# Front of a sequence three ahead in the tail of a step, and pass two's causal mask as a product over 64 rows on TensorE

## The chip, the cores and the metric

One core of one Trainium2 chip. The time is device microseconds of one execution, from the program's first to its last instruction on the core. TensorE is called PE, VectorE DVE, ScalarE ACT, GpSimd POOL and SyncE SP.

## The reference, cut to what matters

32 sequences of 256 tokens with 128 channels go through a layer norm and then through two branches that are added to x: a 16-head attention with rotary positions and a distance bias, and a block with routed projections (8 experts, a gate from cosine similarity), causal attention and a mixture of experts.

```python
xn = layernorm(x)
# branch A: 16 heads of 8 channels
q_rot, k_rot = rotate(q, cos, sin), rotate(k, cos, sin)
scores = q_rot @ k_rot.T / sqrt(8) - |i - j| / xi[h] * e_gate[h]
attn = softmax(where(causal, scores, -inf)); A = (attn @ v) @ Wo.T
# branch B
n1 = layernorm(xn) * ln1_w + ln1_b
rw = gating(n1)                                   # 8 weights a token
q, k, v = sum_e rw[:, e] * (n1 @ proj[e])         # one head of 128
hs = xn + sum_e rw[:, e] * (softmax(causal(q @ k.T) / sqrt(128)) @ v) @ o_proj[e]
n2 = layernorm(hs); B = hs + sum_e rw2[:, e] * gelu(n2 @ w1[e]) @ w2[e]
out = x + A + B
```

## The kernel before, in words

The 32 sequences are worked off by 32 calls of `step(n, u, n_x)` on every engine, one for each sequence n (u is its parity); 26 of them run in a hardware loop of two steps. After them a last stage does the mixture of experts. Each engine has its own program, and its order is written out by hand; engines meet only at semaphores. n_x says how much lies ahead: 3 in steps 0 to 28, 2 in step 29, 1 in step 30, 0 in step 31.

A step mixes three sequences. For n it does branch B's projections (`qk`, `ve`, `soft_scores`, `soft_T`, `soft_av`, `oe`) and branch A's second pass (`unit2`, exponentials, `pv`, `out_T`, `att_T`, `att_out`). For n+1 it does branch A's first pass (`unit1`: scores whose row maxima DVE takes in `row_max`; `max_parts`, `max_T` and `put_max` bring the maxima back into the stacks as rows of pass two). For n+2 it does the front: `norm_T` (transposes of both norms into bank G0), `proj` (q and k with their rotated partners, one after the other through bank G1), `logits_T`, `logits`, `proj_v`, and on DVE `rotate` and `gating`. DVE also makes the layer norm of n+3.

Branch A's scores come in 6 units for each pass. Pass one uses banks S1 (0, 1); a causal mask is put there first by a product of `mask_l` and `mask_r` over the 64 rows of each of two row groups. Pass two uses banks S2 (2, 3); there ACT writes the mask as a seed (`seed_slot`, L669) after each exponential (`exp_slot`, L663), and PE's `unit2` waits for `seed_done`.

DVE's `gating` is a chain of 31 links; each waits for the one before it. Between links stand other pieces of work, at places given by `beside_gating(k)`: one piece of the next layer norm after each link, and row maxima, `normalise`, `soft_max` and `soft_norm` at fixed k. In `layer_norm` the first piece waits for the sequence's x (`x_in`) and then runs `bn_stats` and `bn_aggr` (L881, L884). In the tail DVE runs `max_parts`, `normalise(n, 1)`, five `scale_att`, `add_x` and `add_hs`. `add_hs` ends with the sum `bs` (L1144) that counts `base_done` up.

SP runs all large transfers in one queue. Its step begins like this (L436, L432):

```python
sp_.wait_ge(base_done, n)
if not isinstance(n, int) or n > 0:
    store_base(n - 1, 1 - u)
load_x(n, u, xr, xr_in)
if n_x == 3:
    sp_.wait_ge(x_in, 16 * (n + 3))
    load_x(n + 3, 1 - u, xt, x_in)
```

Lines that the prediction names: `norm_T` L1313, `proj` L1321, `logits` L1334, `proj_v` L1344, `weights_T` L1354, `unit1`'s masks L1371 and L1374, `max_T` L1393, `unit2` L1408 and L1411, `ve` L1458, `soft_T` L1476, `oe` L1493, `att_T` L1501; on DVE `rotate` L987 to L997, `gating` from L1014, `row_max` L1070; on ACT the copy of xnT L617.

Of the kernel before, what the change touches and what calls it, by code (L numbers as in the profile page):

```python
# [15 lines left out]
S = 256  # L16
# [44 lines left out]
GATE_MAX_AT = (7, 12, 17, 22)  # L61
# [58 lines left out]
def build(nc, x, w_attn, w_o, log_xi, pi_logit, e_logit, ln1_w, ln1_b, ln2_w, ln2_b, sim1, gates1,  # L120
# [9 lines left out]
    with ExitStack() as ctx:  # L130
# [9 lines left out]
        mask_in = sb("mask_in", [P, 2, P])  # L140
        mask_half = sb("mask_half", [P, 4, P])
        mask_qk = sb("mask_qk", [P, 2, P], BF16)
        mask_l = sb("mask_l", [P, P], BF16)
# [79 lines left out]
        seeds = trn[:].rearrange("p a t -> p (a t)").bitcast(BF16).rearrange("p (k t) -> p k t", k=2)  # L223
# [16 lines left out]
        S1, S2, PVB, QKB, G0, G1 = (0, 1), (2, 3), 4, 5, 6, 7  # L240

# [42 lines left out]
        seed_done = sem("seed_done")  # L284
# [69 lines left out]
        def _(sp_):  # L354
# [3 lines left out]
            for dst, src in ((ident[:], c_ident), (mask_in[:, 0], c_mask_qk), (mask_in[:, 1], c_mask_kq),  # L358
                             (theta[:], c_pos_freq), (sin_sign[:], c_sin_sign), (cpos[:], c_pos),
                             (rank[:], c_rank), (lnp[:, 0:1], ln1_w), (lnp[:, 1:2], ln1_b),  # L360
                             (lnp[:, 2:3], ln2_w), (lnp[:, 3:4], ln2_b),
                             (sims[:, 0], sim1), (sims[:, 1], sim2)):
                sp_.dma_start(dst, src).then_inc(ld_const, 16)
# [229 lines left out]
        def _(act):  # L593
# [17 lines left out]
            def evac_norm(b, par):  # L611

                act.wait_ge(xzT_out, b + 1)

                if not isinstance(b, int) or b > 1:
                    act.wait_ge(n1s_done, E * (b - 1))
                act.activation(xnT[:], ps[:, G0, 0:S], ACT.Copy).then_inc(xnT_done, 1)  # L617
                act.activation(n1T[:, par], ps[:, G0, S:2 * S], ACT.Identity, bias=lnp[:, 1:2],
                               scale=lnp[:, 0:1]).then_inc(n1T_done, 1)
                act.wait_ge(n1T_done, b + 1)  # L620
                act.activation(sqT[:, 0:S], n1T[:, par], ACT.Square).then_inc(sq_done, 1)
# [18 lines left out]
            def evac_weights(b):  # L640
                act.wait_ge(rwT_out, b + 1)

                act.wait_ge(rw_stored, 16 * b)
                act.activation(rwT[0:E * T, 0:P], ps[0:E * T, S1[1], 0:P], ACT.Copy).then_inc(rwT_done, 1)

            def evac_max(b):
                act.wait_ge(mT_out, b + 1)
                act.wait_ge(max_in, 16 * NF * b)
                act.activation(mT[:], ps[0:3 * H, S1[0], 0:S // 2].bitcast(BF16), ACT.Copy).then_inc(mT_done, 1)
# [22 lines left out]
            def exps(n, k):  # L672
                exp_slot(n, k)
                seed_slot(n, k)
# [84 lines left out]
            def step(n, u, n_x):  # L759
                if n_x >= 2:  # L760
                    evac_norm(n + 2, u)
                exps(n, 0)
# [5 lines left out]
                exps(n, 1)  # L768
# [3 lines left out]
                exps(n, 2)  # L772
# [5 lines left out]
                exps(n, 3)  # L778
                if n_x == 0:
                    scale_norm2(3)  # L780
                exps(n, 4)
# [10 lines left out]
                if n_x:  # L792
                    seed_slot(n, 5)
# [19 lines left out]
            for b in range(2):  # L813
                evac_norm(b, b)
# [3 lines left out]
                evac_weights(b)  # L818
            evac_max(0)
# [50 lines left out]
        def _(dve):  # L870
# [86 lines left out]
            for h in range(2):  # L957
                ch.add(dve.tensor_copy(mask_qk[:, h], mask_in[:, 0]))
# [5 lines left out]
            ch.add(dve.scalar_tensor_tensor(mask_l[:], mask_half[:, 1], FAINT, mask_half[:, 0], ALU.mult, ALU.add))  # L964
            ch.link(dve.memset(seeds[:, 0], 0.0))
            for h in range(2):
                ch.add(dve.tensor_copy(seeds[:, 0, S * h:S * h + P], mask_in[:, 1]))
            ch.add(dve.tensor_copy(seeds[:, 1].rearrange("p (h t) -> p h t", h=HG),
                                   mask_in[:, 1:2].broadcast_to((P, HG, P))))
# [14 lines left out]
            def rotate(b, beside=None):  # L984
                c = Chain(dve, rot_chain, b, ROT_LINKS, beside)
                dve.wait_ge(rot_q_out, b + 1)
                c.link(dve.tensor_tensor(rott[:, 0], ps[:, G1].rearrange("p (a t) -> p a t", a=2), cs[:, 0], ALU.mult))  # L987
                c.add(dve.tensor_tensor(rot[:, 0], rott[:, 0, 0], rott[:, 0, 1], ALU.add))
                dve.wait_ge(rot_k_out, b + 1)
                c.link(dve.tensor_tensor(rott[:, 1], ps[:, G1].rearrange("p (a t) -> p a t", a=2), cs[:, 1], ALU.mult))  # L990
# [187 lines left out]
            def step(n, u, n_x):  # L1178
# [5 lines left out]
                def beside_rotation(k):  # L1184
                    if k == 1:
                        next_max(0)

# [3 lines left out]
                def beside_gating(k):  # L1191
                    next(norm, None)
                    if k in GATE_MAX_AT:
                        next_max(2 + GATE_MAX_AT.index(k))
                    if k == 11:
                        normalise(n, 0)
                    if k == 14:
                        soft_max(n)
                    if k == 20:
                        soft_norm(n)  # L1200
                if n_x >= 2:
                    rotate(n + 2, beside_rotation)
                    next_max(1)
                    gating(n + 2, T, 0, gate1, LG1, NORM1, 1, beside_gating)
                    run(norm)
                else:
                    for k in range(1, ROT_LINKS + 1):
                        beside_rotation(k)
                    next_max(1)
# [13 lines left out]
                add_x(n, u)  # L1223
                add_hs(n, u)

            for b in range(2):
                norm = layer_norm(b + 1, 1 - b)
                rotate(b)
# [4 lines left out]
            max_parts(0)  # L1233
            step(0, 0, 3)
# [61 lines left out]
        def _(pe):  # L1296
# [5 lines left out]
            for j in range(2):  # L1302
                mm(ps[:, S2[j]], identb[:], seeds[:, 0], start=True, stop=False, skip_group_check=True)
            pe.wait_ge(ld_w, 16 * N_W)

            def norm_T(b, free):
# [4 lines left out]
                for k, src in enumerate((xn[:], zt[:])):  # L1311
                    for i in range(T):
                        ins = pe.transpose(ps[:, G0, (T * k + i) * P:(T * k + i + 1) * P], src[:, i], ident[:])  # L1313
                ins.then_inc(xzT_out, 1)

            def proj(b, side, prev):
# [3 lines left out]
                for k in range(2):  # L1320
                    ins = mm(ps[:, G1, k * S:(k + 1) * S], wa[:, 2 * side + k], xnT[:], start=True, stop=True)  # L1321
# [25 lines left out]
            def weights_T(b, old):  # L1347
                pe.wait_ge(rw_out, 3 * (b + 1))
                if old:

                    pe.wait_ge(s1_read, UNITS * b)
                else:
                    pe.wait_ge(rwT_done, b)
                pe.transpose(ps[0:E * T, S1[1], 0:P], gt[:, 6, 0:T].rearrange("p i e -> p (i e)"), ident[:]  # L1354
                             ).then_inc(rwT_out, 1)

            def unit1(b, par, k):

                Q, i = divmod(k, 3)
                if k == 0:  # L1360

                    pe.wait_ge(rwT_done, b + 1 if not isinstance(b, int) or b else 2)
                    pe.wait_ge(mT_done, b)
# [4 lines left out]
                for f in range(NF):  # L1368
                    bank = ps[:, S1[f]]
                    if i == 0:  # L1370
                        mm(bank, mask_l[ROWS[f]], mask_r[ROWS[f]].rearrange("p h t -> p (h t)"), start=True, stop=False,  # L1371
                           skip_group_check=True)
                    else:
                        mm(bank.rearrange("p (h t) -> p h t", h=2)[:, :, P:S], mask_l[ROWS[f]], mask_r[ROWS[f], 0:2],  # L1374
# [13 lines left out]
            def max_T(b):  # L1388

                pe.wait_ge(max_chain, (MAX_LINKS + 1) * (b + 1))  # L1390
                pv = ps[:, S1[0], 0:S // 2].bitcast(BF16)
# [4 lines left out]
            def unit2(n, u, k):  # L1396
# [4 lines left out]
                if not isinstance(n, int) or UNITS * n + k >= 1:  # L1401
                    pe.wait_ge(seed_done, UNITS * n + k)
# [12 lines left out]
            def pv(n, u, Q):  # L1415
# [4 lines left out]
                if Q == 0:  # L1420
                    pe.wait_ge(v_done, n + 1)
                    pe.wait_ge(xa_done, n)
                for f in range(NF):
# [133 lines left out]
            def step(n, u, n_x):  # L1557
                f = n + 2

                def next_max(k):  # L1560
                    if n_x:
                        unit1(n + 1, 1 - u, k)
# [38 lines left out]
                soft_scores(n, (lambda: pe.wait_ge(rot_chain, ROT_LINKS * f + 3)) if n_x >= 2 else  # L1601
                            (lambda: pe.wait_ge(hs_done, n)))
# [4 lines left out]
                next_max(3)  # L1607
# [5 lines left out]
                next_max(4)  # L1613
# [5 lines left out]
                next_max(5)  # L1619
# [3 lines left out]
                if n_x >= 2:  # L1623
                    weights_T(f, True)
                    proj_v(f, True)
                if n_x:
                    max_T(n + 1)

                att_T(n)
                oe(n, 0)  # L1630
                oe(n, 1)
                att_out(n)
                if n_x == 0:
                    weights_T2(0)
                    logits2_T(1)
                for e in range(2, E):
# [4 lines left out]
            for b in range(2):  # L1641

                norm_T(b, lambda: pe.wait_ge(lg_read, b))
                proj(b, 0, lambda: pe.wait_ge(rot_chain, ROT_LINKS * b))
                logits_T(b, b)
                proj(b, 1, lambda: pe.wait_ge(rot_chain, ROT_LINKS * b + 1))
                logits(b)
                proj_v(b, False)
                weights_T(b, False)

            pe.wait_ge(set_dma, 16 * (N_SMALL + N_ROWS))
            for k in range(UNITS):
# [110 lines left out]
```

## Time and profile before

| | us |
|---|---|
| median of 3 runs | 1389.92 |
| lowest, highest | 1386.5, 1391.0 |
| the profiled execution | 1386.97 |
| its span | 1385.1 |
| PE busy | 1229.1 (89%) |
| DVE busy | 1004.5 (73%) |
| ACT busy | 707.4 (51%) |
| POOL busy | 211.0 (15%) |

The steps lie between about 96 and 1142 us of the span, the last stage behind them. Times in the rows are microseconds from the start of the span. In a row of the timeline the first number is the start, the second the time to the end of the last of the merged instructions; "xN" is their count, and a bracket gives how long the engine was idle before the row and which instruction ended that. A PE row's end is modelled, so here the distance from start to start is used for what PE spends on a row.

### The profile page before, as it was taken

The page shows a single profiled execution, that of the slowest core. Times are in us where ns is not written, and L with a number is a line of the kernel's source. Part 1 is how long each engine was busy: PE and PEld are TensorE (multiplying, and loading weights), DVE is VectorE, ACT ScalarE, POOL GpSimd, SP SyncE. Part 2 cuts the span into 40 slices and gives each one's busy share as a digit, 9 for nine tenths or more (in the row PEclk, how much of TensorE's full clock was granted, in tenths as well). Part 3 has the DMA queues.
Part 4 walks back from the last instruction along what each step waited for, and adds up shares of the span by engine and source line. Part 5 has one row for each costly group of instructions (what it writes and reads, how often), then busy time and mean ns, then how long its engine had stood idle before and what let it go on. Part 6 is the DMA issues. An engine that isn't in the chain of part 4 may idle for free.

```text
span 1385.1 us, 33706 instructions
## 1 busy us (share of the span) xinstructions
PE 1229.1 (89%) x10780; PEld 938.4 (68%) x10780; DVE 1004.5 (73%) x3691; ACT 707.4 (51%) x1281; POOL 211.0 (15%) x325
## 2 busy tenths in 40 slices
PE   1249999999999999999999999999999979999998
PEld 0127777777777677777777777777777766777776
DVE  5547777777777777777777777777777657777653
ACT  1115555555555555555555555555555665555532
POOL 1011111121111222221111111112111200000000
PEclk9659999999999999999999999999999999999999
DMA  5312232222222222222322222222222106544344
GB/s 131 87 63 79 79 90 81 82 82 77 78 78 82 81 80 78 77 77 81 96 97 77 77 79 88 81 82 81 80 80 78 53 26 230 194 154 154 154 169 153
DMA packets 107942, 133.19 MB, mean 96 GB/s; under 512 B 18116, under 2 KB 87252, under 8 KB 99692
## 3 DMA queue, kind: packets, MB, share of 16 engines
q1 hardware_dynamic: 105668, 131.66, 29.6%
q10 hardware_dynamic: 2216, 0.80, 0.2%
q8 instruction: 32, 0.52, 0.2%
q14 instruction: 26, 0.21, 0.0%
HBM read 109.12 MB, written 21.54 MB: 94 GB/s over the span
## 4 chain that ended last, share of the span: by engine, by line
PE 68%; DVE 16%; issue 9%; SPq 4%; DMA 2%; ACT 1%; DVEq 0%; ACTq 0%
PE ps L1448 9%; PE ps L1493 9%; PE ps L1694 8%; PE ps L1449 8%; PE ps L1680 8%; PE ps L1321 4%; PE ps L1458 3%; PE ps L1425 2%; DVE mx L1070 2%; PE ps L1408 2%; SPq L415 2%; PE ps L1371 1%; PE ps L1507 1%; PE ps L1381 1%; DVE xn L894 1%
## 5 line engine op out<-in xcount | busy, mean ns | idle before, releaser
L1070 DVE TENSOR_REDUCE mx<-ps 128x4 f32<-128x1024 f32 (+1 forms) x192 | 234.9, 1223 | 89.4 <-PE ps L1381 80.0
L663 ACT ACTIVATE pr<-ps 128x1024 f32<-128x1024 f32 x192 | 195.8, 1020 | 138.4 <-PE ps L1408 93.7
L558 POOL TENSOR_TENSOR n1s<-rep,n1T 128x256 f32<-128x256 f32 x256 | 176.8, 728 | 254.3 <-DVE mpart L1084 254.3
L669 ACT ACTIVATE ps<-trn 128x1024 f32<-128x1024 bf16 x191 | 197.2, 1032 | 5.1
L1694 PEld LDWEIGHTS ps<-w2s,ats 128*128 128x128 f32 x1024 | 131.7, 192 | 49.8 <-issue 46.8
L1448 PE MATMUL ps<-n1s,wqk 128*128 128x256 f32 x512 | 163.0, 400 | 0.0
L1449 PE MATMUL ps<-n1s,wqk 128*128 128x256 f32 x512 | 152.7, 380 | 0.0
L1458 PE MATMUL ps<-wv,n1s 128*128 128x128 f32 x1024 | 141.6, 281 | 0.0
L1493 PE MATMUL ps<-wop,ats 128*128 128x128 f32 x1024 | 140.0, 294 | 0.0
L842 ACT ACTIVATE n1s<-ps 128x512 f32<-128x512 f32 x128 | 76.5, 597 | 122.6 <-PE ps L1680 121.5
L1694 PE MATMUL ps<-w2s,ats 128*128 128x128 f32 x1024 | 135.7, 276 | 0.5 <-DVE ats L1253 0.5
L1458 PEld LDWEIGHTS ps<-wv,n1s 128*128 128x128 f32 x1024 | 126.7, 191 | 11.5 <-issue 6.5
L1493 PEld LDWEIGHTS ps<-wop,ats 128*128 128x128 f32 x1024 | 131.3, 207 | 4.1 <-issue 0.2
L1680 PE MATMUL ps<-rep,w1s 128*128 128x512 f32 x256 | 130.7, 594 | 0.0
L565 POOL TENSOR_TENSOR zt<-xn,rstd 128x256 f32<-128x256 f32 x32 | 19.6, 612 | 638.2 <-DVE rstd L901 638.2
L1449 PEld LDWEIGHTS ps<-n1s,wqk 128*128 128x128 f32 x512 | 97.6, 191 | 13.4
L1448 PEld LDWEIGHTS ps<-n1s,wqk 128*128 128x128 f32 x512 | 87.2, 190 | 25.9 <-issue 12.5
L617 ACT ACTIVATE xnT<-ps 128x256 f32<-128x256 f32 x32 | 12.3, 383 | 162.6 <-PE ps L1313 144.7
L1121 DVE TENSOR_TENSOR ats<-rep,ps 128x512 f32<-128x512 f32 (+1 forms) x160 | 81.2, 574 | 0.0
L1321 PE MATMUL ps<-xnT,wa 128*128 128x256 f32 x256 | 73.4, 412 | 1.6 <-ACT xnT L617 0.9
L1137 DVE SCALAR_TENSOR_TENSOR hs<-ps,smx,hs 128x128 f32 (+1 forms) x64 | 19.5, 347 | 74.2 <-PE ps L1493 74.2
L1425 PE MATMUL ps<-pr,vst 128*32 128x256 f32 x1024 | 68.5, 385 | 0.4 <-ACT pr L663 0.4
(228 smaller groups left out, 2038.3 us busy)
## 6 DMA issues: line engine op xcount, KB each, us to landing
rep<-scr_rw SPq DMA_DIRECT2D x32, 1024.0 KB, 5.0
stk<-scr_rw SPq DMA_DIRECT2D x16, 1024.0 KB, 8.1
stk<-scr_parts SPq DMA_DIRECT2D x896, 16.0 KB
scr_parts<-parts SPq DMA_DIRECT2D x64, 192.0 KB, 2.3
rots<-scr_rw SPq DMA_DIRECT2D x8, 1024.0 KB, 4.8
wqk<-scr_rw SPq DMA_DIRECT2D x8, 1024.0 KB, 8.9
stk<-scr_parts SPq DMA_DIRECT2D x128, 48.0 KB
xt<-in_x SPq DMA_DIRECT2D x32, 128.0 KB, 2.5
```

The lines of the kernel that those rows point to most:

```text
L558: pool.tensor_tensor(n1s[:, e], rep[:, par, e], n1T[:, par], ALU.mult).then_inc(n1s_done, 1)
L663: act.activation(pr[:, Q, :, i], ps[:, S2[0]:S2[0] + NF], ACT.Exp).then_inc(exp_done, 1)
L669: act.activation(ps[:, S2[0]:S2[0] + NF], seeds[:, kind:kind + 1].broadcast_to((P, NF, 512)), ACT.Copy).then_inc(seed_done, 1)
L1070: dve.tensor_reduce(mx[:, min(i, 1)].rearrange("p (f h) -> p f h", f=NF)[:, :, h:h + n], ps[:, S1[0]:S1[0] + NF].rearrange("p f (h t) -> p ...
L1321: ins = mm(ps[:, G1, k * S:(k + 1) * S], wa[:, 2 * side + k], xnT[:], start=True, stop=True)
L1425: mm(ps[32 * h:32 * h + 32, PVB, 0:S], vst[:, u, 0, HH * f + HG * Q + h], pr[:, Q, f, h // 2, (h % 2) * S:(h % 2 + 1) * S], start=(f == 0) ...
L1448: mm(ps[:, QKB, 0:S], wq[:, e], n1s[:, e], start=(e == 0), stop=(e == E - 1), skip_group_check=True)
L1449: ins = mm(ps[:, QKB, S:2 * S], wk[:, e], n1s[:, e], start=False, stop=(e == E - 1), skip_group_check=True)
L1458: ins = mm(ps[:, QKB, i * D:(i + 1) * D], n1s[:, e, i * P:(i + 1) * P], wv[:, e], start=(e == 0 and i == 0), stop=(e == E - 1), skip_group ...
L1493: ins = mm(ps[:, G1, i * D:(i + 1) * D], ats[:, e, i * P:(i + 1) * P], wop[:, e], start=(e == 0 and i == 0), stop=(e == E - 1), skip_group ...
L1680: mm(ps[:, UP[k % 4]], w1s[:, e], n2T[t % 8], start=True, stop=True).then_inc(up_out, 1)
L1694: ins = mm(ps[:, MOE[t % 2], i * D:(i + 1) * D], hgs[:, k % 2, i * P:(i + 1) * P], w2s[:, e], start=(e == 0 and i == 0), stop=(e == E - 1) ...
```

## The change

1. The front of a sequence is worked three ahead in place of two ahead. In steps 0 to 28, `norm_T(n+3)` and `proj(n+3, 0)` (q) stand in PE's tail behind `proj_v(n+2)`, and `proj(n+3, 1)` (k) behind `oe(n, 3)`. They use the banks `LATER` = S1[0] for the transposes, S1[1] for q, PVB for k, where before it was G0, G1, G1. ACT's `evac_norm` is split: xnT is copied in the tail (`evac_norm_x`), n1T and its square at the start of the next step (`evac_norm_1`). DVE's `rotate(n+3)` stands between `add_x(n)` and `add_hs(n)`. The start of the step loses them. The setup does the same once for sequence 2, and step 29 has no front of its own to transpose or project.
2. `weights_T` and `max_T` go to bank G1 in place of S1, and PE waits for ACT's copies of both (`rwT_done`, `mT_done`) ahead of `oe(n, 0)`, which writes the same bank. `evac_weights` waits for `mT_out`.
3. Pass two's mask is a product on PE (`mask_r` as the stationary side, `mask_q` as the moving one) ahead of each `unit2`; `seed_slot` and its semaphore go, and `unit2` waits for the exponential of the unit before.
4. The six row maxima of n+1 all stand beside the gating chain, at k = 2, 7, 11, 16, 20, 24; before, two stood beside or behind `rotate` and four at k = 7, 12, 17, 22. `soft_max` moves from k = 14 to 17, `normalise(n, 0)` from 11 to 18, `soft_norm` from 20 to 28. PE's `unit1` calls move with them, 2 to 5 each to an earlier place.
5. The setup loses two seeds' tiles and PE's two products with them, and one constant load. SP's program is as before but for that load.

```diff
-GATE_MAX_AT = (7, 12, 17, 22)
+GATE_MAX_AT = (2, 7, 11, 16, 20, 24)
+        FIRST, LATER = (G0, G1, G1), (S1[0], S1[1], PVB)
@@ ACT
-            def evac_norm(b, par):
+            def evac_norm_x(b, banks):
                 act.wait_ge(xzT_out, b + 1)
+                act.activation(xnT[:], ps[:, banks[0], 0:S], ACT.Copy).then_inc(xnT_done, 1)
+            def evac_norm_1(b, par, banks):
...
             def evac_weights(b):
                 act.wait_ge(rwT_out, b + 1)
+                if not isinstance(b, int) or b > 1:
+                    act.wait_ge(mT_out, b)
...
-            def seed_slot(n, k):
-                act.wait_ge(exp_done, UNITS * n + k + 1)
-                kind = 1 if (k + 1) % 3 == 2 else 0
-                act.activation(ps[:, S2[0]:S2[0] + NF], seeds[:, kind:kind + 1].broadcast_to((P, NF, 512)), ACT.Copy
-                               ).then_inc(seed_done, 1)
...
                 evac_pv(n, 1)
                 if n_x >= 2:
+                    evac_v(n + 2, u)
+                if n_x == 3:
+                    evac_norm_x(n + 3, LATER)
+                if n_x >= 2:
                     evac_weights(n + 2)
-                    evac_v(n + 2, u)
@@ DVE
                 def beside_gating(k):
                     next(norm, None)
                     if k in GATE_MAX_AT:
-                        next_max(2 + GATE_MAX_AT.index(k))
-                    if k == 11:
+                        next_max(GATE_MAX_AT.index(k))
+                    if k == 17:
+                        soft_max(n)
+                    if k == 18:
                         normalise(n, 0)
-                    if k == 14:
-                        soft_max(n)
-                    if k == 20:
+                    if k == 28:
                         soft_norm(n)
                 if n_x >= 2:
-                    rotate(n + 2, beside_rotation)
-                    next_max(1)
                     gating(n + 2, T, 0, gate1, LG1, NORM1, 1, beside_gating)
...
                 add_x(n, u)
+                if n_x == 3:
+                    rotate(n + 3, LATER)
                 add_hs(n, u)
@@ PE, unit2
-                    pe.wait_ge(seed_done, UNITS * n + k)
+                    pe.wait_ge(exp_done, UNITS * n + k)
+                for f in range(NF):
+                    bank = ps[:, S2[f]]
+                    if i < 2:
+                        mm(bank.rearrange("p (h t) -> p h t", h=2)[:, :, 0:P], mask_r[ROWS[f], 0],
+                           mask_q[ROWS[f], 0:2], start=True, stop=False, skip_group_check=True)
+                    else:
+                        mm(bank, mask_r[ROWS[f], 0], mask_q[ROWS[f]].rearrange("p h t -> p (h t)"),
+                           start=True, stop=False, skip_group_check=True)
@@ PE, step
-                if n_x >= 2:
-                    norm_T(f, lambda: pe.wait_ge(ats_done, len(ATS_CHUNKS) * n))
                 unit2(n, u, 0)
                 qk(n, 0)
-                if n_x >= 2:
-                    proj(f, 0, lambda: pe.wait_ge(hs_done, n))
                 qk(n, 1)
...
                 if n_x >= 2:
-                    proj(f, 1, lambda: pe.wait_ge(rot_chain, ROT_LINKS * f + 1))
                     logits(f)
...
                 qk(n, 6)
+                next_max(2)
                 qk(n, 7)
-                pv(n, u, 0)
+                pv(n, u, 0, f if n_x >= 2 else None)
-                next_max(2)
+                next_max(3)
                 unit2(n, u, 3)
...
                 soft_T(n)
-                next_max(5)
                 pv(n, u, 1)
                 soft_av(n, (lambda: pe.wait_ge(lg_read, f + 1)) if n_x >= 2 else (lambda: None))
                 out_T(n, 1)
                 if n_x >= 2:
-                    weights_T(f, True)
                     proj_v(f, True)
+                if n_x == 3:
+                    norm_T(g, LATER, lambda: pe.wait_ge(s1_read, UNITS * f))
+                    proj(g, 0, LATER, lambda: None)
+                if n_x >= 2:
+                    weights_T(f, lambda: None)
                 if n_x:
                     max_T(n + 1)
                 att_T(n)
+                if n_x >= 2:
+                    pe.wait_ge(rwT_done, f + 1)
+                if n_x:
+                    pe.wait_ge(mT_done, n + 2)
                 oe(n, 0)
                 oe(n, 1)
                 att_out(n)
+                oe(n, 2)
+                oe(n, 3)
+                if n_x == 3:
+                    proj(g, 1, LATER, lambda: pe.wait_ge(xa_done, n + 1))
-                for e in range(2, E):
+                for e in range(4, E):
                     oe(n, e)
```

Here f is n+2 and g is n+3.

## Rows read from the trace of the kernel before

**Rows 1.** The page, engine totals: busy us, share of the span, instructions.
```profile
PE 1229.1 (89%) x10780; PEld 938.4 (68%) x10780; DVE 1004.5 (73%) x3691; ACT 707.4 (51%) x1281; POOL 211.0 (15%) x325
```
**Rows 2.** Timeline of PE: the first and last full step, and one step's sparse part.
```profile
129.63 0.38 PE L1313 MATMUL ps<-ident,xn 128*128 128x128 f32 x2
...
622.48 0.38 PE L1313 MATMUL ps<-ident,xn 128*128 128x128 f32 x2
...
642.57 0.71 PE L1458 MATMUL ps<-wv,n1s 128*128 128x128 f32 x4
643.95 0.55 PE L1476 MATMUL ps<-ident,sp 128*128 128x128 f32 x3 [0.67 <-ACT sp L690]
644.71 0.28 PE L1374 MATMUL ps<-mask_r,mask_l 64*128 64x256 bf16 x2 [0.21 <-DVE mx L1070]
...
647.34 0.38 PE L1437 MATMUL ps<-ident,ov 128*128 128x128 f32 x2
649.02 0.27 PE L1354 MATMUL ps<-ident,gt 128*16 128x128 f32 x1 [1.30 <-DVE gt L1051]
...
649.80 0.29 PE L1393 MATMUL ps<-identb,mpart 128*128 128x128 bf16 x2
650.36 0.44 PE L1501 MATMUL ps<-ident,att 128*128 128x128 f32 x2 [0.27 <-DVE att L1096]
...
652.13 2.84 PE L1493 MATMUL ps<-wop,ats 128*128 128x128 f32 x24
654.81 0.38 PE L1313 MATMUL ps<-ident,xn 128*128 128x128 f32 x2
...
1045.95 0.38 PE L1313 MATMUL ps<-ident,xn 128*128 128x128 f32 x2
```
**Rows 3.** Timeline of PE: a mask of pass one, then the logits and `unit1(1)`.
```profile
627.54 0.39 PE L1371 MATMUL ps<-mask_r,mask_l 64*128 64x512 bf16 x2
627.77 0.39 PE L1381 MATMUL ps<-stk 64*128 64x128 bf16 x8
...
629.27 0.27 PE L1334 MATMUL ps<-ident,lgT 128*128 128x128 f32 x1
...
631.21 0.28 PE L1374 MATMUL ps<-mask_r,mask_l 64*128 64x256 bf16 x2
```
**Rows 4.** The page, costliest groups: count, busy us, mean ns, idle before.
```profile
L669 ACT ACTIVATE ps<-trn 128x1024 f32<-128x1024 bf16 x191 | 197.2, 1032 | 5.1
```
**Rows 5.** Timeline of ACT: the copy of xnT at a step's start.
```profile
655.52 0.38 ACT L617 ACTIVATE xnT<-ps 128x256 f32<-128x256 f32 x1 [4.31 <-PE ps L1313]
```
**Rows 6.** Timeline of DVE: `add_hs` ends, `rotate`'s second half, gating begins.
```profile
623.46 0.42 DVE L1144 TENSOR_TENSOR bs<-hs,xa 128x256 f32<-128x256 f32 x1
...
629.77 0.68 DVE L990 TENSOR_TENSOR rots<-ps,cs 128x512 f32<-128x512 f32 x1
...
633.29 1.22 DVE L1070 TENSOR_REDUCE mx<-ps 128x4 f32<-128x1024 f32 x1
...
634.50 0.48 DVE L881 BATCH_NORM_STATS2 bst<-xt 128x6 f32<-128x128 f32 x2
...
635.47 0.16 DVE L103 SCALAR_TENSOR_TENSOR gs<-gs 128x2 f32<-128x2 f32 x1
```
**Rows 7.** Timeline of SP's queue: the first transfers of a step.
```profile
624.08 0.39 SPq L436 DMA_DIRECT2D scr_base<-bs  x1
...
625.35 0.39 SPq L432 DMA_DIRECT2D xt<-in_x  x1
```
**Rows 8.** The page, DMA issues: KB each, median us from issue to landing.
```profile
xt<-in_x SPq DMA_DIRECT2D x32, 128.0 KB, 2.5
```
**Rows 9.** Timeline of DVE in the setup.
```profile
67.63 0.49 DVE L881 BATCH_NORM_STATS2 bst<-xt 128x6 f32<-128x128 f32 x2 [7.47 <-DMA xt<-in_x]
```
**Rows 10.** Busy time and granted clock of two stretches (start:end, length, engines, PEclk).
```profile
316.30:318.80 2.50, 1.26 (x9) 0.92 (x9) 2.22 (x14) 0.94 (x4) 0.73 (x2) 1.00 0.24 51
318.80:322.30 3.50, 3.50 (x18) 3.37 (x18) 2.61 (x6) 0.41 (x2) 3.50 (x6) 0.51 0.15 33
```

More of the change, by code:

```diff
@@ L963, in _ @@
                                             mask_half[:, 2:3].broadcast_to((P, HG, P)), ALU.mult, ALU.add))
[L964 to L969, printed above, removed]
+            ch.add(dve.scalar_tensor_tensor(mask_q[:], mask_half[:, 1:2].broadcast_to((P, HG, P)), FAINT,
+                                            mask_half[:, 0:1].broadcast_to((P, HG, P)), ALU.mult, ALU.add))
             ch.add(dve.tensor_copy(identb[:], ident[:]))
@@ L982, in _, with rotate @@
             ch.close()
[L984 to L985 removed]
+            def rotate(b, banks):
+                c = Chain(dve, rot_chain, b, ROT_LINKS)
+                half = "p (a t) -> p a t"
                 dve.wait_ge(rot_q_out, b + 1)
[L987 removed]
+                c.add(dve.tensor_tensor(rott[:, 0], ps[:, banks[1]].rearrange(half, a=2), cs[:, 0], ALU.mult))
+                c.wait()
                 c.add(dve.tensor_tensor(rot[:, 0], rott[:, 0, 0], rott[:, 0, 1], ALU.add))
                 dve.wait_ge(rot_k_out, b + 1)
[L990 removed]
+                c.add(dve.tensor_tensor(rott[:, 1], ps[:, banks[2]].rearrange(half, a=2), cs[:, 1], ALU.mult))
+                c.wait()
                 c.link(dve.tensor_tensor(rot[:, 1], rott[:, 1, 0], rott[:, 1, 1], ALU.add))
@@ L1233, in _ @@
             max_parts(0)
+            rotate(2, LATER)
             step(0, 0, 3)
@@ L1301, in _, with norm_T @@
             pe.wait_ge(set_dve, N_SET_DVE)
-            for j in range(2):
-                mm(ps[:, S2[j]], identb[:], seeds[:, 0], start=True, stop=False, skip_group_check=True)
             pe.wait_ge(ld_w, 16 * N_W)
-            def norm_T(b, free):
+            def norm_T(b, banks, free):
                 free()
@@ L1312, in norm_T, with proj @@
                     for i in range(T):
-                        ins = pe.transpose(ps[:, G0, (T * k + i) * P:(T * k + i + 1) * P], src[:, i], ident[:])
+                        ins = pe.transpose(ps[:, banks[0], (T * k + i) * P:(T * k + i + 1) * P], src[:, i], ident[:])
                 ins.then_inc(xzT_out, 1)
-            def proj(b, side, prev):
+            def proj(b, side, banks, prev):
                 pe.wait_ge(xnT_done, b + 1)
@@ L1320, in proj @@
                 for k in range(2):
-                    ins = mm(ps[:, G1, k * S:(k + 1) * S], wa[:, 2 * side + k], xnT[:], start=True, stop=True)
+                    ins = mm(ps[:, banks[1 + side], k * S:(k + 1) * S], wa[:, 2 * side + k], xnT[:], start=True, stop=True)
                 ins.then_inc((rot_q_out, rot_k_out)[side], 1)
@@ L1345, in proj_v, with weights_T, unit1 @@
                 ins.then_inc(v_out, 1)
-            def weights_T(b, old):
+            def weights_T(b, free):
                 pe.wait_ge(rw_out, 3 * (b + 1))
[L1349 to L1354, printed above, removed]
+                free()
+                pe.transpose(ps[0:E * T, G1, 0:P], gt[:, 6, 0:T].rearrange("p i e -> p (i e)"), ident[:]
                              ).then_inc(rwT_out, 1)
-            def unit1(b, par, k):
+            def unit1(b, par, k, front=None):
                 Q, i = divmod(k, 3)
-                if k == 0:
-                    pe.wait_ge(rwT_done, b + 1 if not isinstance(b, int) or b else 2)
-                    pe.wait_ge(mT_done, b)
+                if k == 0 and front is not None:
+                    pe.wait_ge(n1T_done, front + 1)
+                    pe.wait_ge(rot_chain, ROT_LINKS * front + 1)
                 if i == 0:
@@ L1422, in pv @@
                     pe.wait_ge(xa_done, n)
+                    if front is not None:
+                        pe.wait_ge(rot_chain, ROT_LINKS * front + 3)
                 for f in range(NF):
@@ L1653, in _ @@
                 unit1(0, 0, k)
+            norm_T(2, LATER, lambda: pe.wait_ge(s1_read, UNITS))
+            proj(2, 0, LATER, lambda: None)
+            pe.wait_ge(rwT_done, 2)
             max_T(0)
+            proj(2, 1, LATER, lambda: None)
             step(0, 0, 3)
```

82 lines of the change are left out of this document (35 added, 47 removed).

## Prediction

> **What bounds the kernel now.** I read the engine totals first, then PE's timeline over one step, then what each of its gaps waits for, then the timelines of DVE, ACT and SP over the same step. The totals say PE, busy 89% of the span [rows 1]. Its timeline shows a step of 32.33 us, from 622.48 to 654.81 [rows 2]; the first three quarters of it have no gap at all, and what idles is the tail. From start to start, and taking off what a row issues (0.44 us for one expert of `ve`, 0.33 for three transposes, 0.21 for two, 0.54 for `weights_T` and `proj_v` together, 0.11 for `max_T`), the gaps are 0.94 us ahead of `soft_T`, 0.43 ahead of `unit1(5)`, 1.47 ahead of `weights_T` at 649.02, 0.24 ahead of `max_T`, 0.45 and 0.1 around `att_T`: about 3.6 us a step. The largest ones are DVE's, the end of the gating chain and what follows it. So the kernel is PE-bound with a DVE tail that costs it some 3 us a step; ACT is half idle, so what the seeds cost ACT costs the kernel nothing now.
>
> 28 steps take 1045.95 - 129.63 = 916.3 us, 32.73 each [rows 2]. The 0.40 above 32.33 is the clock: after a sparse stretch (PE busy 1.26 of 2.5 us) a stretch follows at a granted 0.51, that is at 1.2 in place of 2.4 GHz, with PE busy throughout [rows 10]. A stretch of 3.5 us at half rate costs at most 1.75 us, so the 11.2 us lost in 28 steps are seven to nine such stretches.
>
> **The change part by part.**
>
> *The mask on PE.* The seeds go: six a step of 1.03 us on ACT [rows 4]. No PE row waits for one in the steps shown, so that saves nothing. Six pairs of products come. The same form is in pass one: from the mask at 627.54 to what follows at 627.77 are 0.23 us for 512 columns in both row groups [rows 3], so 0.12 for 256. A step has four of 256 and two of 512: 4 x 0.12 + 2 x 0.23 = **+0.94 us** on the engine that bounds. The Trainium skill says in "TensorEngine Tiling (Array Packing)", section Theoretical Speedup, that a contraction of up to 64 rows can run as two tiles side by side for up to twice the rate; by that the pair costs one product's time, which is what the row shows, and without it this term would be 1.9 us.
>
> *The gaps of the new order, if all data is there in time.* I walked PE's list with the start-to-start times of the rows.
> - `unit1(1)` waits for `row_max(0)`, now behind k = 2 of gating. Gating can start 0.3 us after `logits` starts; the place behind k = 2 comes 1.04 us later (0.07 for its first link and 0.97 from 634.50 to 635.47, the first piece of the layer norm among them) [rows 6]; the maximum takes 1.22, PE wakes 0.06 later: 2.6 us. PE has 631.21 - 629.27 = 1.94 us of work there [rows 3]. Gap 0.7.
> - `pv(n, 1)` follows `soft_T` directly; the exponential of unit 5 takes as long as a seed, 1.03 [rows 4], plus 0.1 to start and wake. Beside it lie 0.44 + 0.33 and the end of the unit: gap 0.4. `soft_T` itself waits no more.
> - `proj(g, 0)` follows `norm_T(g)` directly: the copy of xnT starts 0.71 after the first transpose and takes 0.38 [rows 2, 5], so PE goes on 1.15 after `norm_T` began, where 0.43 is its own: gap 0.7.
> - `oe(n, 0)` waits for ACT's copies of weights and maxima, one after the other behind `max_T`: about 1.0 after `max_T` starts (0.4 for ACT to see it, as `norm_T` and its copy show, then 0.2 and 0.38 [rows 5]), with 0.32 of PE work beside it: gap 0.7.
> - DVE's gating ends well ahead of `weights_T` now: it starts some 7 us earlier in the step and has two more maxima (2.3 us) within.
>
> Sum 2.5 in place of 3.6. Step: 32.33 - 3.6 + 2.5 + 0.94 = 32.2. So far the change is worth **-0.1 us** a step: one microsecond of gaps traded for one of masks. Each of the four gaps is uncertain by 0.2, the sum by 0.5.
>
> *Where data is not there in time.* Moved together, two things meet: gating starts early and `base_done` comes late. SP starts its step only at `base_done`, and the x that `layer_norm(n+3)` wants is SP's third transfer. The layer norm's first piece stands behind link 1 of gating, in DVE's queue; if x is missing, DVE stands there with `row_max(0)`, and with it `unit1(1)` and all of PE.
> - Before: `bs` ends at 623.88, SP issues the store at 624.08 and x at 625.35 [rows 6, 7], it lands 2.5 later [rows 8] at 627.85, and `bn_stats` runs at 634.50 [rows 6]. 6.6 us to spare.
> - After, counted from the start E of the step (end of `oe(7)`): `proj(g, 1)` starts 0.86 + 4/6 x 2.68 = 2.65 before E (four experts of the six that take 652.13 to 654.81 [rows 2]); `rotate`'s second half can start 1.06 behind that, at E - 1.59. It lasts 3.52 (629.77 to 633.29 [rows 6]), to E + 1.9. `add_hs` then takes 0.65 to its sum and 0.42 more: `base_done` at E + 3.05, where it was E + 1.4. SP wakes at +0.2, issues x 1.27 later at E + 4.5, and x lands at **E + 7.0**.
> - Gating can start behind `logits`. PE's list ahead of that, from starts of rows, is unit2(0) 0.44, three `qk` 3.0, `logits_T` 0.35, unit1(0) 0.45, unit2(1) 0.43: E + 4.7, and DVE starts at **E + 5.0**, then stands for 2.0 us. `row_max(0)` runs from E + 8.0 (0.97 behind `bn_stats` [rows 6]) to 9.2, PE goes on at E + 9.3. Without the wait it would have gone on at E + 7.3, without any gap at 6.6.
>
> Such a wait can be seen in the setup, where the same `bn_stats` stood 7.47 us for x with the gating chain behind it [rows 9]. The shift repeats in each step, since `base_done` is tied to the step's end. Price: +1.9 us, step 34.1, **+1.8 over before**. It applies to steps 1 to 28 (step 0 waits for no `base_done`, step 29 has no layer norm): 28 x 1.8 = **+50 us**. Landing between 2.2 and 3 us, SP's wake and the walk's error leave 1.3 to 2.3 a step, 36 to 64 us.
>
> *The clock.* The new hole is 2.7 us (E + 6.6 to 9.3) with nothing in it, longer than any now. In the rows a stretch with half its time idle was enough for half rate behind it, in about one step of four [rows 2, 10]. What the hole does lies between -11 (the tail's sparse stretch is broken up and nothing falls) and 28 x 1.75 - 11 = +38 us (each step). I take two steps of three: 18 x 1.4 - 11 = **+13 us**, nearer to the upper end because the hole is emptier than the stretch that did it before. The Trainium skill's "TensorE: Matmul & The Clock Gate", Part 1, says that the clock follows how busy PE has lately been; this speaks against any change that gathers idle time into one hole, and the rows agree.
>
> *Ends.* `max_T(0)` now stands behind `norm_T(2)` and `proj(2, 0)` in the setup, some 2.5 us at the half clock that holds there; step 29 lacks those same instructions and gives it back. Other edits (banks, the split copy on ACT, `proj_v` ahead of `weights_T`) move work within slack of more than 1 us. 0, within 5.
>
> **Sum.** 1387.0 (the profiled execution) + 50 + 13 = 1450. That execution lies 2.9 below the median of the three runs, so for a median: **1453 us**, 4.5% slower.
>
> **The rivals.**
> 1. *x is there in time.* If `rotate`'s tail is shorter than I read it, or gating starts later than `logits` allows, the DVE wait goes. Then 28 x -0.1 and the clock from -11 to +10: 1377 to 1397, likeliest 1387. This is the other side of the forecast. It decides at E + 5: x must land 2 us earlier than I work out, or gating start 2 us later. For it: `row_max(0)` and the layer norm have 6.6 us to spare now. Against: the 6.6 are spent by 6.9 (gating's earlier start) plus 1.7 (the later `base_done`). Chance 12%, half of it faster by more than 0.3%.
> 2. *The tail's gaps close altogether.* Without the x wait and with PE at its own work, 28.7 + 0.94 a step: 1387 - 28 x 2.7 = 1312 at the very best, 1350 with half of it. Against: four waits have ACT or DVE directly between two PE instructions. Chance 5%.
> 3. *Half clock behind every hole.* Everything as forecast, but 28 stretches: 1387 + 50 + 38 + 3 = 1478. [...] Chance 8%.
> 4. *The forecast*, 1422 to 1475: chance 75%.
>
> **How the numbers follow.** Faster by over 0.3% (about what a measurement of this kernel can tell from no change): half of rival 1 and rival 2, 0.11. Within 0.3%: 0.06. Slower: 0.83. The range leaves out rivals 1 and 2 and the far end of 3: 1412 to 1480; the low end is 1387 + 36 - 11, the high end 1387 + 50 + 38 + 5.
>
> **What would show it.** Right: DVE's `bn_stats` idle about 2 us "<- DMA xt" in steps 1 to 28; PE's pass-one mask row ahead of `unit1(1)` idle about 2.5 us, released by the `row_max` line; steps of 34 us and more; `base_done`'s sum 3 us behind the last `oe`; gaps of 0.7 ahead of `proj(g, 0)` and `oe(n, 0)`; the seeds' line gone and six mask rows of 0.12 and 0.23; half-clock stretches right behind the hole, more than nine. Wrong: no wait for xt, or one hidden because PE waits longer for something else, such as the stack's transfers; then the first thing to read is who releases `unit1(1)`.

## The result and the profile after

The changed kernel takes 1460.66 us (median of 4, 1456.09 to 1463.45), the kernel before 1389.76: a ratio of 1.0511, 95% interval 1.0477 to 1.0545, 71 us slower. The profiled execution took 1462.25 us, 75.3 above that of before. Forecast were 1453 us and a range of 1412 to 1480.

The page of the kernel after, engine totals as in [rows 1], and the lines that answer to [rows 4, 8]:

```profile
PE 1257.2 (86%) x11162; PEld 950.7 (65%) x11162; DVE 1015.6 (70%) x3687; ACT 518.8 (36%) x1090; POOL 211.8 (15%) x325
...
L666 ACT ACTIVATE pr<-ps 128x1024 f32<-128x1024 f32 x192 | 196.7, 1024 | 391.9 <-PE ps L1399 222.0
...
xt<-in_x SPq DMA_DIRECT2D x32, 128.0 KB, 2.7
```

No seed is left (L666 are the exponentials). ACT has 189 us less work and the kernel gains nothing by it; PE works 28 us more within a span that is 75 longer. So PE now idles in places where it did not. The timeline of PE in the kernel after, one step of 34.56 us, from `unit2(0)`'s mask at 667.53 to the next at 702.09, with what stands before it:

```profile
656.22 1.07 PE L1419 MATMUL ps<-pr,vst 128*32 128x256 f32 x16 [0.23 <-ACT pr L666]
...
660.16 1.13 PE L1307 MATMUL ps<-xnT,wa 128*128 128x256 f32 x4 [0.47 <-ACT xnT L612]
...
661.35 0.39 PE L1496 MATMUL ps<-ident,att 128*128 128x128 f32 x2
662.45 1.15 PE L1488 MATMUL ps<-wop,ats 128*128 128x128 f32 x8 [0.72 <-ACT mT L652]
...
667.53 0.28 PE L1389 MATMUL ps<-mask_q,mask_r 64*128 64x256 bf16 x2
...
672.17 0.33 PE L1320 MATMUL ps<-ident,lgT 128*128 128x128 f32 x1
...
673.63 0.59 PE L1443 MATMUL ps<-n1s,wqk 128*128 128x256 f32 x2
676.93 0.28 PE L1356 MATMUL ps<-mask_r,mask_q 64*128 64x256 bf16 x2 [2.70 <-DVE mx L1064]
...
702.09 0.28 PE L1389 MATMUL ps<-mask_q,mask_r 64*128 64x256 bf16 x2
```

The tail that waited for DVE in [rows 2] is closed: no wait ahead of `weights_T`. In its place stand three waits for ACT, ahead of `pv(n, 1)` (0.23 us), `proj(g, 0)` (0.47) and `oe(n, 0)` (0.72), and the hole of 2.70 us ahead of `unit1(1)`, the largest idle time of a step. Its releaser is the row maximum on L1064. The timelines of DVE and of SP's queue in the same step say what held that maximum up:

```profile
670.02 0.42 DVE L1138 TENSOR_TENSOR bs<-hs,xa 128x256 f32<-128x256 f32 x1
672.54 0.16 DVE L1008 TENSOR_SCALAR gs<-ps 128x2 f32<-128x2 f32 x1 [2.09 <-PE ps L1320]
674.54 0.49 DVE L876 BATCH_NORM_STATS2 bst<-xt 128x6 f32<-128x128 f32 x2 [1.85 <-DMA xt<-in_x]
...
675.65 1.23 DVE L1064 TENSOR_REDUCE mx<-ps 128x8 f32<-128x1024 f32 x1
```
```profile
670.65 0.39 SPq L435 DMA_DIRECT2D scr_base<-bs  x1
671.23 0.41 SPq L431 DMA_DIRECT2D xr<-in_x  x1
671.92 0.39 SPq L431 DMA_DIRECT2D xt<-in_x  x1
```

The first link of gating runs 5.0 us into the step, the next instruction in DVE's queue stands 1.85 us for x. Over the execution DVE waited 63.9 us for it, in 29 places, one of them 8.1 us in the setup, so 2.0 us a step in steps 1 to 28:

```profile
DVE bst L876 <- DMA xt<-in_x: 63.9, 29, 8.1
```

Steps 1 to 28 reach from the first of these rows to the second:

```profile
131.51 0.28 PE L1389 MATMUL ps<-mask_q,mask_r 64*128 64x256 bf16 x2
...
1124.02 0.28 PE L1389 MATMUL ps<-mask_q,mask_r 64*128 64x256 bf16 x2
```

They take 992.5 us, 35.45 each, where it was 32.73 [rows 2]. In 17 of them the granted clock is full throughout, and these average 34.52 us. The other 11 hold 47.7 us at half clock (3.4 us in eight of them, 6.8 in three); before, 9 steps held 30.7 us. In all 11 the half clock begins 8 to 11 us into the step, within or just behind the hole. One of the three longest, in step 14, looks like this; busy time and granted clock of three stretches around it (start:end, length, PE, PEld, DVE, ACT, POOL, PEclk, DMA share, GB/s):

```profile
600.00:603.00 3.00, 2.02 (x11) 1.47 (x9) 0.16 (x1) 1.03 (x1) 0.00 (x0) 1.00 0.66 213
603.00:604.80 1.80, 0.00 (x0) 0.00 (x0) 1.52 (x8) 0.00 (x0) 0.00 (x0) 0.83 0.86 323
604.80:608.20 3.40, 2.62 (x19) 1.78 (x20) 3.40 (x18) 0.90 (x1) 0.00 (x0) 0.50 0.45 142
```

PE does nothing from 603.00 to 604.80 while DVE works at what x released, and the stretch behind runs at 0.50, that is at 1.2 in place of 2.4 GHz. The length of the hole alone does not tell which step is hit: it lies between 2.2 and 3.6 us in steps 1 to 27, four holes of more than 3.0 us had full clock behind them, and two of 2.43 and 2.45 us did not.

### The profile page after: what moved, and what is told of

Same layout as the page of the kernel before. It is cut to its first block, busy times and chain, and to the rows that moved or that the text cites. A ratio compares the mean times of both kernels' runs of the same rounds, so it can differ in the third digit from the quotient of the medians.

```text
span 1460.4 us, 34320 instructions
## 1 busy us (share of the span) xinstructions
PE 1257.2 (86%) x11162; PEld 950.7 (65%) x11162; DVE 1015.6 (70%) x3687; ACT 518.8 (36%) x1090; POOL 211.8 (15%) x325
## 4 chain that ended last, share of the span: by engine, by line
PE 64%; DVE 13%; DMA 7%; SPq 6%; ACT 4%; issue 4%; DVEq 1%; ACTq 0%
PE ps L1699 8%; PE ps L1685 7%; PE ps L1452 7%; DMA xt<-in_x 5%; PE ps L1442 5%; PE ps L1488 5%; PE ps L1419 4%; PE ps L1307 4%; PE ps L1443 4%; DVE mx L1064 3%; ACT pr L666 2%; PE ps L1356 2%; PE ps L1366 2%; PE ps L1424 2%; SPq L414 2%
## 5 line engine op out<-in xcount | busy, mean ns | idle before, releaser
L666 ACT ACTIVATE pr<-ps 128x1024 f32<-128x1024 f32 x192 | 196.7, 1024 | 391.9 <-PE ps L1399 222.0
L1064 DVE TENSOR_REDUCE mx<-ps 128x4 f32<-128x1024 f32 (+1 forms) x192 | 234.8, 1223 | 75.9 <-PE ps L1366 68.3
L1442 PE MATMUL ps<-n1s,wqk 128*128 128x256 f32 x512 | 175.2, 425 | 0.0
L1443 PE MATMUL ps<-n1s,wqk 128*128 128x256 f32 x512 | 162.6, 401 | 0.0
L1488 PE MATMUL ps<-wop,ats 128*128 128x128 f32 x1024 | 133.9, 279 | 19.7 <-ACT mT L652 17.9
L1488 PEld LDWEIGHTS ps<-wop,ats 128*128 128x128 f32 x1024 | 125.1, 193 | 28.6 <-DVE ats L1115 24.0
L1443 PEld LDWEIGHTS ps<-n1s,wqk 128*128 128x128 f32 x512 | 103.4, 202 | 15.8
L1356 PE MATMUL ps<-mask_r,mask_q 64*128 64x256 bf16 x256 | 37.9, 292 | 85.1 <-DVE mx L1064 85.1
L1442 PEld LDWEIGHTS ps<-n1s,wqk 128*128 128x128 f32 x512 | 90.6, 202 | 31.0 <-issue 21.6
L1356 PEld LDWEIGHTS ps<-mask_r,mask_q 64*128 64x128 bf16 x256 | 12.4, 94 | 119.9 <-DVE mx L1064 98.5
L1307 PEld LDWEIGHTS ps<-xnT,wa 128*128 128x128 f32 x256 | 46.6, 203 | 28.8 <-ACT xnT L612 23.2
```

The source lines that it names most:

```text
L666: act.activation(pr[:, Q, :, i], ps[:, S2[0]:S2[0] + NF], ACT.Exp).then_inc(exp_done, 1)
L1064: dve.tensor_reduce(mx[:, min(i, 1)].rearrange("p (f h) -> p f h", f=NF)[:, :, h:h + n], ps[:, S1[0]:S1[0] + NF].rearrange("p f (h t) -> p ...
L1307: ins = mm(ps[:, banks[1 + side], k * S:(k + 1) * S], wa[:, 2 * side + k], xnT[:], start=True, stop=True)
L1442: mm(ps[:, QKB, 0:S], wq[:, e], n1s[:, e], start=(e == 0), stop=(e == E - 1), skip_group_check=True)
L1443: ins = mm(ps[:, QKB, S:2 * S], wk[:, e], n1s[:, e], start=False, stop=(e == E - 1), skip_group_check=True)
L1488: ins = mm(ps[:, G1, i * D:(i + 1) * D], ats[:, e, i * P:(i + 1) * P], wop[:, e], start=(e == 0 and i == 0), stop=(e == E - 1), skip_group ...
```

## The experiments

All ratios are to runs of the kernel before on the same chip. The theory: x for the layer norm comes too late for a DVE that now starts gating early, and this costs 1.8 us a step. Its rival: the early row maximum, or another of SP's transfers, holds the step anyway.

**x issued first.** SP's step begins with the load of x for n+3, behind a wait for the layer norm that last read the buffer, which was done two steps ago.

```diff
+                if n_x == 3:
+                    sp_.wait_ge(ln_out, n + 2)
+                    sp_.wait_ge(x_in, 16 * (n + 3))
+                    load_x(n + 3, 1 - u, xt, x_in)
                 sp_.wait_ge(base_done, n)
                 if not isinstance(n, int) or n > 0:
                     store_base(n - 1, 1 - u)
                 load_x(n, u, xr, xr_in)
-                if n_x == 3:
-
-                    sp_.wait_ge(x_in, 16 * (n + 3))
-                    load_x(n + 3, 1 - u, xt, x_in)
```

> The changed kernel with one edit on SP: the load of x for the layer norm of n+3 is issued first in the step, behind a wait for the layer norm that last read its buffer, and no longer behind base_done. Theory (DVE stands about 2 us a step for x, and PE with it): the wait of bn_stats for x goes, the gap ahead of unit1(1) falls from 2.5-2.7 to 0.5-0.7 us, a step without a clock dip takes 32.6 in place of 34.5 us, and with fewer half-clock stretches the time is 1385 to 1405 us. Rival (the gap ahead of unit1(1) is the early row maximum's own, or another transfer of SP's takes the place of x): above 1440 us.

1387.69 us, ratio 0.9983 (0.997 to 0.9995). One edit of four lines off DVE and PE gives 73 us back. The wait for x is gone but for the one in the setup, and the hole is a third of what it was. Its wait line, then PE's timeline:

```profile
DVE bst L876 <- DMA xt<-in_x: 8.5, 1, 8.5
```
```profile
627.75 0.33 PE L1320 MATMUL ps<-ident,lgT 128*128 128x128 f32 x1
...
629.21 0.59 PE L1443 MATMUL ps<-n1s,wqk 128*128 128x256 f32 x2
630.71 0.28 PE L1356 MATMUL ps<-mask_r,mask_q 64*128 64x256 bf16 x2 [0.91 <-DVE mx L1064]
```

A step takes 32.78 us (32.74 and 32.83 in turn), 1.78 less than the 34.56 of the step shown above, and no stretch of the 28 steps falls to half clock. The forecast's step for this case was 32.2.

**The same edit on the kernel before**, as a control.

> A control: the kernel before with x issued first in SP's step, the same edit as in x_first. Theory (there x has 6.6 us to spare, so the edit is worth nothing by itself and what it gave back in x_first was the changed kernel's wait): 1384 to 1394 us, no difference. Rival (the edit frees SP's queue or the store of the base and helps any kernel): faster by more than 0.5%.

1388.75 us, ratio 1.0002 (0.999 to 1.0015). The edit is worth nothing by itself: what it gave back above was the changed kernel's own wait.

**add_hs ahead of the rotation.**

```diff
                 add_x(n, u)
+                add_hs(n, u)
                 if n_x == 3:
                     rotate(n + 3, LATER)
-                add_hs(n, u)
```

> The changed kernel with add_hs ahead of rotate(n+3) on DVE, so that base_done is 1.9 us earlier against the step's end and the rotation that much later. Theory: x lands at about 5.4 us of the step in place of 7.0, but DVE is busy with the rotation until 5.7, so gating's first piece runs at 5.7 in place of 7.0: 1.3 us a step, 1410 to 1430 us. Rival (late x is not what holds the step): 1455 us or more, since DVE does the same work.

1409.14 us, ratio 1.0138 (1.0113 to 1.0164), 1 us under the range expected. `base_done` comes earlier, x is there, and DVE is late for another reason, its rotation, as DVE's timeline shows:

```profile
635.74 0.42 DVE L1138 TENSOR_TENSOR bs<-hs,xa 128x256 f32<-128x256 f32 x1
...
640.07 0.69 DVE L991 TENSOR_TENSOR parts<-rots,parts 128x512 bf16<-128x512 f32 x1
640.68 0.15 DVE L1008 TENSOR_SCALAR gs<-ps 128x2 f32<-128x2 f32 x1
640.77 0.49 DVE L876 BATCH_NORM_STATS2 bst<-xt 128x6 f32<-128x128 f32 x2
```

Gating and the layer norm start 1.17 us behind `logits` (639.51), with no wait between them; with x first, the hole ahead of `unit1(1)` is 0.91 us, here it is 1.60. A step takes 33.48 us. The place of one addition in DVE's tail was thus worth 50 us, through a store that nobody in the step reads.

**x issued later**, behind the spread weights and the parts.

```diff
-                if n_x == 3:
-
-                    sp_.wait_ge(x_in, 16 * (n + 3))
-                    load_x(n + 3, 1 - u, xt, x_in)
                 if n_x:
                     spread_weights(n + 1, 1 - u)
                 if n_x >= 2:
                     store_parts(n + 2, u)
+                if n_x == 3:
+
+                    sp_.wait_ge(x_in, 16 * (n + 3))
+                    load_x(n + 3, 1 - u, xt, x_in)
```

> The changed kernel with the load of x for n+3 issued behind the spreading of the weights and the two stores of the parts, about 1.4 us later in SP's queue. Theory: the wait of bn_stats for x grows by as much as the issue moves, 1.4 us, and each of the 28 steps with it: 1490 to 1515 us (or more, if the 1 MB of the spread weights slows the load down). Rival (x is not on the path): within 5 us of the changed kernel's 1461.

1621.03 us, ratio 1.1678 (1.163 to 1.1726): the direction of the theory, but 160 us in place of the 30 to 55 I had worked out. Issue to landing grew too. SP's queue, then DVE and PE of one step:

```profile
669.08 0.38 SPq L425 DMA_DIRECT2D rep<-scr_rw  x1
669.58 0.90 SPq L396 DMA_DIRECT2D scr_parts<-parts  x2
670.74 0.52 SPq L431 DMA_DIRECT2D xt<-in_x  x1
```
```profile
676.42 0.49 DVE L876 BATCH_NORM_STATS2 bst<-xt 128x6 f32<-128x128 f32 x2 [6.40 <-DMA xt<-in_x]
```
```profile
678.80 0.40 PE L1356 MATMUL ps<-mask_r,mask_q 64*128 64x256 bf16 x2 [7.26 <-DVE mx L1064]
```

x now takes 5.7 us from issue to landing, where it took 2.6 in the changed kernel: it is issued 1.7 us behind the 1 MB of spread weights, in the same queue. That the queue's order holds it up is not shown apart from the load on the DMA engines, which are busy throughout from 671 to 675.5 (DMA share 1.00). DVE's wait rises from 1.85 to 6.40 us, 4.55 more, of which 1.5 are the later issue and 3.1 the slower load. A step takes 40.95 us, 6.4 more than 34.56; the 1.85 beyond the wait are PE's work at half clock behind a hole of 7.26 us (the row itself, 0.40, was 0.28), now in every step. The granted clock right behind the hole of this step:

```profile
678.80:681.00 2.20, 2.20 (x18) 1.44 (x19) 2.20 (x13) 0.48 (x1) 0.00 (x0) 0.50 0.00 0
```

**The masks alone.** The kernel before with products for pass two's masks and no seeds; the rest as it was.

```diff
             def exps(n, k):
                 exp_slot(n, k)
-                seed_slot(n, k)
...
-                    pe.wait_ge(seed_done, UNITS * n + k)
+                    pe.wait_ge(exp_done, UNITS * n + k)
+                for f in range(NF):
+                    bank = ps[:, S2[f]]
+                    if i < 2:
+                        mm(bank.rearrange("p (h t) -> p h t", h=2)[:, :, 0:P], mask_r[ROWS[f], 0],
+                           mask_q[ROWS[f], 0:2], start=True, stop=False, skip_group_check=True)
+                    else:
+                        mm(bank, mask_r[ROWS[f], 0], mask_q[ROWS[f]].rearrange("p h t -> p (h t)"),
+                           start=True, stop=False, skip_group_check=True)
```

> The kernel before with pass two's mask as products on PE and no seeds on ACT, nothing else changed. Theory A (the 0.94 us a step of my sum lie on PE's path in full): 32 steps x 0.94 = +30 us, 1415 to 1422 us. Theory B (the part behind the start of DVE's gating chain is taken up by PE's gap ahead of weights_T, which waits for that chain): +0.3 to 0.4 us a step, 1398 to 1404 us. Theory C (the seeds were on the path): no slower than before.

1399.07 us, ratio 1.0066 (1.0042 to 1.009): 9 us, theory B's number. But the gap that gave way was only in part the one B named. PE's timeline:

```profile
650.44 0.55 PE L1477 MATMUL ps<-ident,sp 128*128 128x128 f32 x3 [0.35 <-ACT sp L690]
...
655.38 0.27 PE L1347 MATMUL ps<-ident,gt 128*16 128x128 f32 x1 [1.17 <-DVE gt L1046]
```

The gap ahead of `weights_T` is 1.17 where [rows 2] has 1.30, and the one ahead of `soft_T` 0.35 where it was 0.67. ACT is not what moved there: its exponentials for the softmax wait for DVE's `smx` with the seeds (first row, the kernel before, 20.5 us into the step) and without them (second row, 21.0 us in).

```profile
642.99 0.37 ACT L688 ACTIVATE sp<-ps,smx 128x128 f32<-128x128 f32 x1 [0.72 <-DVE smx L1108]
```
```profile
649.47 0.37 ACT L688 ACTIVATE sp<-ps,smx 128x128 f32<-128x128 f32 x1 [0.94 <-DVE smx L1103]
```

So PE with its masks gets to `soft_T` later, and waits less there for a chain that comes through DVE. Together 0.45 of the 0.9 us are taken up; a step takes 32.70 where undisturbed ones before take 32.22.

**Seeds kept.** x issued first, and pass two's masks left to ACT, so the early front with the row maxima moved along.

> x_first (x issued first in SP's step, 1387.7 us) with the mask of pass two given back to ACT's seeds, so the early front alone. Theory (with x there in time PE is the bound again, and the masks lie on its path): a step of 32.78 us loses 0.94 and may get back up to 0.7 where a seed delays the exponentials ahead of soft_T: 1361 to 1382 us. Rival (as in the kernel before, DVE's chain takes up what PE spends on masks): 1383 us or more.

1369.65 us, ratio 0.9858 (0.9832 to 0.9884). A step takes 32.18 us, 0.60 less than with products; the wait for the exponential ahead of `pv(n, 1)` doubles to 0.45 (it was 0.23) and takes most of the rest. So the products cost 18 us here and 9 in the kernel before. And the early front, with x in time, makes the kernel 1.4% faster, though its step of 32.18 us is no shorter than an undisturbed one before (32.22): steps 1 to 28 take 900.2 us in place of 916.3, and nearly all of that are the 9 steps with half clock, of which it has none.

**A reordered tail**, on x issued first.

```diff
                     norm_T(g, LATER, lambda: pe.wait_ge(s1_read, UNITS * f))
-                    proj(g, 0, LATER, lambda: None)
                 if n_x >= 2:
                     weights_T(f, lambda: None)
                 if n_x:
                     max_T(n + 1)
                 att_T(n)
+                if n_x == 3:
+                    proj(g, 0, LATER, lambda: None)
```

> x_first with weights_T, max_T and att_T moved between norm_T(g) and proj(g, 0) on PE: the two ACT waits of the new tail (0.65 ahead of proj, 0.89 ahead of oe(0), start to start) then lie beside PE work. Theory: 0.43 us of PE work goes into the first gap, 0.96 us (proj) into the second: 0.65 + 0.89 - 0.22 = 1.3 us a step less, 1349 to 1356 us. Rival (DVE's or POOL's chain is just behind these gaps): 1375 us or more.

1347.39 us, ratio 0.9694 (0.9668 to 0.9719). The ACT waits ahead of `proj(g, 0)` and `oe(n, 0)` are gone from PE's timeline, and of the step's brackets two are left, here in the order of time:

```profile
640.24 0.28 PE L1356 MATMUL ps<-mask_r,mask_q 64*128 64x256 bf16 x2 [0.88 <-DVE mx L1064]
654.15 1.07 PE L1419 MATMUL ps<-pr,vst 128*32 128x256 f32 x16 [0.23 <-ACT pr L666]
```

A step takes 31.39 us, 1.39 less. In each of the two gaps a PE instruction had stood directly behind ACT's copy of the result of the one before.

**All of it**: x first, seeds on ACT, the reordered tail.

> x_first with both edits: seeds on ACT in place of masks on PE, and the reordered tail. Theory: both gains add up, 1322 to 1345 us. Rival (a DVE chain becomes the bound once PE has 2 us less): 1350 us or more.

1331.11 us, ratio 0.9579 (0.9554 to 0.9604). A step takes 30.79; the gains add up.

**All, with `unit1(1)` behind `qk(5)` and `unit1(2)` behind `qk(7)`.**

```diff
                 qk(n, 4)
-                next_max(1)
                 unit2(n, u, 2)
                 qk(n, 5)
+                next_max(1)
...
                 qk(n, 6)
-                next_max(2)
                 qk(n, 7)
+                next_max(2)
```

> As all, and unit1(1) behind qk(5), unit1(2) behind qk(7), so that the first row maximum has one expert's 0.86 us more of PE work beside it. Theory: the gap ahead of unit1(1), 1.07 us start to start in x_first, falls to 0.2: 0.8 us a step less than all, 1300 to 1323 us. Rival (the row maxima then run late and the gap reappears at unit1(3) or ahead of weights_T): within 8 us of all.

1318.31 us, ratio 0.9491 (0.9463 to 0.9518), 71 us under the kernel before, 142 under the changed one. The brackets of PE's timeline in one step:

```profile
634.49 0.28 PE L1378 MATMUL ps<-mask_r,mask_q 64*128 64x256 bf16 x2 [0.21 <-DVE mx L1084]
636.41 1.07 PE L1433 MATMUL ps<-pr,vst 128*32 128x256 f32 x16 [0.23 <-ACT pr L668]
...
652.96 0.40 PE L1416 MATMUL ps<-stk 64*128 64x128 bf16 x8 [0.19 <-ACT ps L674]
```

The step is 30.3 us, 0.45 under that of "all" where the wait ahead of `unit1(1)` (0.88 there) could have given 0.8. The time lies in the theory's range, but part of the gap came back, as the rival had it: 0.21 stand now ahead of `unit1(5)` and 0.19 ahead of a `unit2`, for a seed.

## Why the prediction was right, and where a term was off

The mechanism is shown: take the late x away and 73 us go, put it later and the step grows by the wait, and the same edit does nothing where x had time to spare. Point by point:

- *The wait for x, +1.8 us a step, +50 us.* Measured: 34.52 us for the steps at full clock less 32.75 for those of the kernel with x first, 1.8 us a step and 50 in 28. The walk in parts: `bs` ends 2.9 us into the step (forecast 3.05), x is issued at 4.4 (4.5), lands at 7.0 (7.0), gating starts at 5.0 (5.0), PE goes on at 9.4 (9.3). All of it could be read in [rows 2, 6, 7, 8], since no instruction of this path was new; only the places were.
- *The step with x in time, -0.1 us.* This term was mis-sized: 32.75 against 32.20 for the undisturbed steps before, so +0.55, some 15 us in 28 steps. 0.13 of the error is the base: the sum started from 32.33, the longer one of two kinds of step that take turns (32.12 and 32.33). The rest is in the gaps: the one ahead of `unit1(1)` is 1.07 us from start to start in the kernel with x first (forecast 0.7), the one ahead of `oe(n, 0)` 0.83 there and 0.89 in the changed kernel (0.7), and `proj(g, 0)` takes 0.96 where I had 0.86. Two of the four gaps came out as forecast: 0.39 ahead of `pv` (0.4) and 0.65 ahead of `proj` (0.7).
- *The masks, +0.94.* The rows are 0.11 and 0.21 to 0.23 us, 0.9 a step. On the path they were 0.48 (before) and 0.60 (x first): PE then waits less elsewhere, which I had not counted.
- *The clock, +13 us.* (18 x 1.4 - 11, as written, is 14.) Taking 28 steps at full clock off, the clock cost 15 us in 28 steps before (916.3 - 28 x 32.20) and 26 after (992.5 - 28 x 34.52), so +11. The size is right and its parts are partly luck: I had taken 18 steps, 11 were hit, and they cost 2.4 us each in place of 1.4, since three held twice the time at half clock. With the hole at 0.9 us (x first) none was hit. What decides which hole is followed by half clock stays open.
- *Ends, 0.* 50 + 15 + 11 = 76 against 75 between the two profiled executions; the ends give 1 back.
- Together: 1450 + 15 - 2 - 1 = 1462 is the profiled execution of after. The 3 us that I added for the median were not needed, since that execution lies 1.6 above its own median; so 1453 stands against 1461.
- Rival 1 (x in time) is what "x issued first" runs as: 1388, where 1387 had been worked out. That is luck: +15 for the gaps and -15 for a clock that never fell cancel. Rival 2 (the tail's gaps close) did not come about in the change, and the reordered tail shows that it took an edit of its own. Rival 3 (half clock behind every hole) came in the kernel with x later, where the hole was 7.26 us.

## What to carry to other kernels

When a consumer is moved earlier, list what its engine's queue will ask for next, not just what the moved work itself reads, and date each of these from its own trigger; here a piece of a layer norm between two links was the one that had lost its slack, by 6.9 us from the one side and 1.6 from the other. A transfer should wait for the last reader of its buffer and for nothing else: x hung on a semaphore of an unrelated store ahead of it in the queue. And an instruction that reads another engine's copy of the result just before it wants other work in between; two such pairs were worth 40 us.

## What the runs showed of the hardware that I had not expected

A load of 128 KB issued 1.7 us behind a 1 MB broadcast on the same queue landed 5.7 us after its issue, not 2.6. Products of a mask over 64 rows on PE (0.9 us a step) cost half of themselves in one schedule and two thirds in the other. A kernel whose PE gaps were at most 0.9 us (x first) kept the full clock through all 28 steps. The kernel before fell to half clock in nine of the same steps, each time in its tail, behind gaps of at most 1.3 us; that cost it 15 us, where the early front with seeds shortened these steps by 16. The changed kernel, with one hole of 2.2 to 3.6 us, fell in eleven.
